# An AdaLN feed-forward kernel in split fp32r: the small transfers of pair 0 on GpSimd's queue, pair 0's blocks used in another order, and two reorderings on VectorE and ScalarE

## What is computed

```python
att = softmax(mlp(cond_128))                     # 64 x 8
agg_w = einsum('bk,koi->boi', att, weight)       # a 64 x 64 matrix per sample
y = einsum('boi,bih->boh', agg_w, x) + (att @ bias_k)[:, :, None]
scores = y @ gate_w.T + gate_b                   # 4 ranks
lora = y @ A[:r].T @ B[:, :r].T                  # r = the rank with the largest score
out = x + y @ W.T + b + lora
```

## Time and profile before

| | us |
|---|---|
| runs timed | 458.45, 458.93, 459.08 (median 458.93) |
| profiled execution, its time | 458.18 |
| its span on the core | 456.3 |
| PE busy | 450.4 (99%) |
| DVE busy | 343.8 (75%) |
| ACT busy | 181.4 (40%) |
| POOL busy | 19.4 (4%) |
| chain that ended last: PE, DVE, ACT | 96%, 3%, 1% |

### The profile page before, as it was taken

One profiled execution on the slowest core, in us unless ns is written; L12 is line 12 of the kernel. 1 busy time (PEld: TensorE's weight loads), 2 busy tenths in 40 slices (PEclk: granted clock), 3 DMA queues, 4 the chain that ended last, 5 costly groups with the idle time before them and its releaser, 6 DMA issues.

```text
span 456.3 us, 10477 instructions
## 1 busy us (share of the span) xinstructions
PE 450.4 (99%) x3510; PEld 445.8 (98%) x3510; DVE 343.8 (75%) x889; ACT 181.4 (40%) x415; POOL 19.4 (4%) x46
## 2 busy tenths in 40 slices
PE   9999999899999999999999999999999999999997
PEld 7999999899999999999999999999999999999997
DVE  4887988799586876958687695868769586876945
ACT  5654554455243343524334342433334243342511
POOL 1010000010000000000000000000000000100000
PEclk9999999999999999999999999999999999999999
DMA  7973560711608053250805235080523408052202
GB/s 273 344 277 54 145 227 1 239 46 52 232 1 278 6 188 97 88 195 0 281 1 194 88 90 192 0 278 4 201 81 108 174 5 277 0 190 95 92 2 93
DMA packets 23773, 59.18 MB, mean 130 GB/s; under 512 B 6862, under 2 KB 8834, under 8 KB 23684
## 3 DMA queue, kind: packets, MB, share of 16 engines
q1 hardware_dynamic: 23508, 58.78, 39.0%
q10 hardware_dynamic: 240, 0.07, 0.1%
HBM read 40.69 MB, written 18.15 MB: 129 GB/s over the span
## 4 chain that ended last, share of the span: by engine, by line
PE 96%; DVE 3%; ACT 1%; issue 0%; POOL 0%; ACTq 0%; POOLq 0%
PE p_p L1071 74%; PE p_o L1089 4%; PE p_o L1091 4%; PE p_o L1109 3%; PE p_o L1090 3%; PE p_o L1108 3%; PE p_p L1115 1%; PE p_p L1136 1%; PE p_p L1097 1%; PE p_o L1136 1%; DVE wl L716 1%; DVE w_raw L722 1%; DVE zl L792 0%; DVE aggw L776 0%; DVE prod L773 0%
## 5 line engine op out<-in xcount | busy, mean ns | idle before, releaser
L1071 PE MATMUL p_p<-wh,xh 128*128 128x274 f32 (+1 forms) x880 | 256.6, 292 | 0.0
L1071 PE MATMUL p_p<-wh,xl 128*128 128x274 f32 (+1 forms) x880 | 254.2, 289 | 0.0
L1071 PE MATMUL p_p<-wl,xh 128*128 128x272 f32 (+1 forms) x864 | 250.5, 290 | 0.0
L1071 PEld LDWEIGHTS p_p<-wh,xh 128*128 128x128 f32 x880 | 166.5, 189 | 0.4 <-issue 0.4
L1071 PEld LDWEIGHTS p_p<-wh,xl 128*128 128x128 f32 x880 | 166.7, 189 | 0.1
L1071 PEld LDWEIGHTS p_p<-wl,xh 128*128 128x128 f32 x864 | 163.0, 189 | 0.1
L579 ACT ACTIVATE zh<-sv 128x274 fp32r<-128x274 f32 (+1 forms) x56 | 24.3, 433 | 95.0 <-DVE sv L804 95.0
L811 DVE TENSOR_TENSOR xin<-p_o,xin 128x274 f32<-128x274 f32 (+2 forms) x128 | 52.0, 418 | 2.7 <-PE p_o L1109 1.9
L557 ACT ACTIVATE xh<-s_raw 128x512 fp32r<-128x512 f32 x60 | 36.3, 628 | 17.1 <-DVE s_raw L759 16.4
L579 ACT ACTIVATE zh<-p_p 128x272 fp32r<-128x272 f32 (+1 forms) x44 | 17.5, 398 | 60.7 <-PE p_p L1071 59.0
L766 DVE TENSOR_TENSOR xl<-s_raw,xh 128x512 fp32r<-128x512 f32 x60 | 40.9, 682 | 0.1
(11 more groups left out here) (140 smaller groups left out, 508.4 us busy)
## 6 DMA issues: line engine op xcount, KB each, us to landing
xin<-in_x SPq DMA_DIRECT2D x32, 512.0 KB, 4.0
raw<-in_xt SPq DMA_DIRECT2D x31, 512.0 KB, 5.2
out<-xin SPq DMA_DIRECT2D x30, 512.0 KB, 5.9
w_raw<-in_w SPq DMA_DIRECT2D x8, 274.0 KB, 7.0
w_raw<-in_w SPq DMA_DIRECT2D x8, 272.0 KB, 6.0
g_aggw<-aggw_all SPq DMA_DIRECT2D x8, 128.0 KB, 2.4
aggw<-g_aggw SPq DMA_DIRECT2D x15, 64.0 KB, 5.0
out<-xin SPq DMA_DIRECT2D x4, 137.0 KB, 2.1
```

Source lines behind the costliest of these rows:

```text
L1071: last = nc.tensor.matmul(o[:, 0:W[r]], a, m, start=start and p == 0, stop=stop and p == 2, skip_group_check=True)
```

## The change

**a. Pair 0 on PE and the weights' order.** The first round's blocks come as B12, B22, B11, B21. Its units stand so that each A block with the same weight block follows at once: `first_unit` B12, `other_unit`, `first_unit` B22, `attention_rows`, `other_unit`, `first_unit` B11 with `attention_products` in its middle, `other_unit`, `first_unit` B21; then the mixes of Z12 and Z22, the last unit, the mix of Z11, and round 1's first two units before the mix of Z21. The two `keep_busy(2)` inside the first `first_unit`s go. Column sums 0 and 1 swap.

**b. Transfers.** All 28 small ones are issued by POOL; SP's loads of `raw` are split in halves and `kern_s` comes before `kern`.

**c. ACT's and DVE's lists of pair 0** follow the new order; `kern_h` moves from DVE to ACT.

**d. Pair 2 on DVE.** `t_sum(0, R11)` comes before `bd_lo` of tile 1, and `z_lo` of Z11 right behind that, ahead of the residual and of the second `t_sum`.

**e. The end on PE.** The last mix and lora (Z21) are written out so that only the matmul with `zl` follows `z_lo`.

```diff
-        W_ORDER = [(r, n, h) for r in range(2) for n in (B11, B21, B12, B22) for h in range(2)]
+        W_ORDER = [(r, n, h) for r, blocks in enumerate(((B12, B22, B11, B21), (B11, B21, B12, B22)))
+                   for n in blocks for h in range(2)]
...
 # POOL
+            pool.wait_ge(s_kern_hl, 2)
+            for n, rows in enumerate((kern_h, kern_l)):
+                pool.dma_start(g_kern[n].rearrange("k (a n) -> (k a) n", n=KC), rows[:, :].bitcast(F32)).then_inc(s_k_stored, 16)
+            pool.wait_ge(s_aggbt, 1)
...
             u_bias(0, 0)
             u_bias(0, 1)
+            pool.wait_ge(s_k_stored, 16 * 2)
+            for h in range(HALVES):
+                for g, n in enumerate((0, 1, 0, 0)):
+                    row = (h * GROUPS + g) * K
+                    pool.dma_start(k_rows[row:row + K, :].bitcast(F32),
+                                 g_kern[n][:, h * KHALF:(h + 1) * KHALF]).then_inc(s_k_rows, 16)
+            pool.wait_ge(s_b_lo, 1)
+            for n, rows in enumerate((b_h, b_l)):
+                pool.dma_start(g_b[n].rearrange("(a o) -> a o", o=P), rows).then_inc(s_b_stored, 16)
+            sum_rows(0)
+            sum_rows(1)
+            pool.wait_ge(s_b_stored, 16 * 2)
+            pool.dma_start(bt_l[ROW_BH:ROW_BL + 1, :].bitcast(F32), g_b).then_inc(s_rows[0], 16)
+            sum_rows(2)
+            sum_rows(3)
...
 # DVE, pair 0
+            w_lo(6)
             mixing_weights(0)
+            w_lo(7)
+            z_lo(0, 0, 0, Z12)
             mixing_weights(1)
+            bd_lo(0, 0, 0)
+            z_lo(0, 0, 0, Z22)
+            bd_lo(0, 0, 1)
             cs_lo(0)
...
+            cs_lo(1)
+            z_lo(0, 0, 0, Z11)
...
 # PE, pair 0
                 if kk % 2 == 0:
-                        if at < 2:
-                            keep_busy(2)
                         pe.wait_ge(s_wl, at + 1)
...
-            first_unit(0, 0, 0)
+            first_unit(0, 2, 0, 0)
             pe.wait_ge(s_al, 2)
-            first_unit(0, 0, 1)
+            other_unit(0, 1, 0)
+            pe.wait_ge(s_al, 3)
+            first_unit(0, 2, 1, 1)
             attention_rows()
-            pe.wait_ge(s_al, 3)
-            first_unit(0, 1, 0, attention_products)
             pe.wait_ge(s_al, 4)
-            first_unit(0, 1, 1)
-            other_unit(0, 2, 0)
-            other_unit(0, 2, 1)
+            other_unit(0, 1, 1)
+            first_unit(0, 0, 0, 2, attention_products)
             other_unit(0, 3, 0)
-            mix(0, 0, 0, Z11)
-            other_unit(0, 3, 1)
-            pe.wait_ge(s_cs_lo, 2)
-            mix(0, 0, 0, Z22)
+            first_unit(0, 0, 1, 3)
             pe.wait_ge(s_aggbt, 2)
             pe.wait_ge(s_aggb, 1)
             mix(0, 0, 0, Z12)
-            first_unit(1, 0, 0)
-            first_unit(1, 0, 1)
+            pe.wait_ge(s_cs_lo, 1)
+            mix(0, 0, 0, Z22)
+            other_unit(0, 3, 1)
+            mix(0, 0, 0, Z11)
+            first_unit(1, 0, 0, 4)
+            first_unit(1, 0, 1, 5)
+            pe.wait_ge(s_cs_lo, 2)
             mix(0, 0, 0, Z21)
...
 # DVE, step
+                if two:
+                    t_sum(0, R11, R12, R11)
                 bd_lo(i, j, 1)
+                if two:
+                    z_lo(i, j, 0, Z11)
                 if not one:
                     residual(i, j - 1, 1, Z21)
                 if two:
-                    t_sum(0, R11, R12, R11)
                     t_sum(0, R12, R22, R12)
...
 # PE, the end
+            pe.wait_ge(s_zh, piece(*last, 1, Z21))
+            pe.wait_ge(s_y, piece(*last, 1, Z21 - 4))
+            nc.tensor.matmul(o, bd[:, 1, 0, :], zh[:, 1, zs], start=True, stop=False)
+            nc.tensor.matmul(o, bd[:, 1, 1, :], zh[:, 1, zs], start=False, stop=False)
+            nc.tensor.matmul(o, ut_hl[:, mine], bt_h[:, cols], start=False, stop=False)
+            nc.tensor.matmul(o, ut_h1[0:ROWS, mine], bt_l[0:ROWS, cols], start=False, stop=False)
+            pe.wait_ge(s_zl, piece(*last, 1, Z21))
+            nc.tensor.matmul(o, bd[:, 1, 0, :], zl[:, 1, zs], start=False, stop=True).then_inc(s_lora, 1)
```

More of the change, by code:

```diff
@@ L321, in piece, with made, z_place @@
             return count(i, j, PIECES, 4 * r + n)
+        def made(i, j, r, n):
+            return piece(i, j, r, MADE[n] if is_pair(i, j, 0) and r == 0 else n)
+        def z_place(i, j, r, n):
+            return (made(0, 0, 0, n) if is_pair(i, j, 0) and r == 0 else n) % 2 ^ 1
         def a_count(i, j, n):
@@ L401, in mixing_weights @@
                 sp.dma_start(aggw[:, :, :], g_aggw_pair[i * 2 + j]).then_inc(s_aggw_in, 16)
+            for t in range(4):
+                sp.dma_start(xin[:, t, :], x_t[t]).then_inc(s_x_in[t], 16)
             sp.wait_ge(s_g_stored, 16 * 3)
             gate_rows(0, 0)
[L405 to L422, removed]
             for n in range(KCH):
@@ L571, in z_hi @@
                 if early(i, j, r) or n == Z11:
-                    act.wait_ge(s_z, product(i, j, r, n if early(i, j, r) else P2))
+                    act.wait_ge(s_z, product(i, j, r, made(0, 0, 0, n) if is_pair(i, j, 0) and r == 0
+                                             else n if early(i, j, r) else P2))
                     src = {Z11: pa, Z22: pb, Z12: pc, Z21: pd}[n][:, 0:W[r]]
@@ L606, in _ @@
             w_hi(1)
+            act.wait_ge(s_raw_a21_in, 16)
+            nc.scalar.activation(a21h[:, :], raw[:, 1, 0:HB], ACT.Copy).then_inc(s_x1h, 1)
             act.wait_ge(s_sm, 4)
@@ L612, in _ @@
             act.wait_ge(s_raw_in[1], 16)
-            nc.scalar.activation(a21h[:, :], raw[:, 1, 0:HB], ACT.Copy).then_inc(s_x1h, 1)
             nc.scalar.activation(xh[:, A22, :], raw[:, 1, HB:H], ACT.Copy).then_inc(s_x1h, 1)
-            for m in range(4, 10):
-                w_hi(m)
+            w_hi(4)
+            w_hi(5)
+            act.wait_ge(s_kern_s_in, 16)
+            nc.scalar.activation(kern_h[:, :], kern_s[:, :], ACT.Copy).then_inc(s_kern_hl, 1)
+            z_hi(0, 0, 0, Z12)
+            w_hi(6)
+            w_hi(7)
+            z_hi(0, 0, 0, Z22)
             cs_hi(0)
-            z_hi(0, 0, 0, Z11)
+            w_hi(8)
+            w_hi(9)
             act.wait_ge(s_clear, 5)
@@ L988, in step @@
                     s_lo(i, j, S3)
-                z_lo(i, j, 0, Z11)
+                if not two:
+                    z_lo(i, j, 0, Z11)
                 if one:
@@ L1354, with blocks @@
     low = (half + 3) // 4 * 2
[L1356 to L1358 removed]
+    def blocks(cols, halves):
+        parts = [wag[k:k + kh, :, c + cols.start:c + cols.stop] for c in halves for k in (0, kh)]
         return np.stack([np.reshape(w, (2, kh // 2, P, -1)).transpose(0, 2, 1, 3) for w in parts])
@@ L1369 @@
         "bias_k": layer["bias_k"],
-        "w0": blocks(slice(low, half)),
-        "w1": blocks(slice(0, low)),
+        "w0": blocks(slice(low, half), (half, 0)),
+        "w1": blocks(slice(0, low), (0, half)),
         "b": ffn["b"],
```

153 lines of the change are left out of this document (73 added, 80 removed).

## The result

The changed kernel takes 462.63 us (median of 6 runs, 461.62 to 464.48) against 458.69 (6 runs, 458.40 to 459.20): a ratio of 1.0091, 95% interval 1.0066 to 1.0115. It is slower by 3.9 us, and PE waits where the prediction said; the sizes of the terms came out otherwise. Its profiled execution took 461.90 us with a span of 459.9, 3.6 us more than before. Single executions of one kernel differ by some us, and their granted clocks differ with them; that turns out to be part of the story.

The account below looks back on a forecast made before the run. PE, busy 99% of the span, was taken to bound the kernel. 458.18 + 0.2 (start) + 7.3 (transfers) + 1.0 (clock) - 1.4 (pair 2) - 0.5 (end) = 464.8; with 0.75 to the median, 465.5 us, range 457.0 to 471.0.

Parts of the forecast that it names:

- The place: POOL's queue held by `u_bias(0, 1)` to 34.53; PE waits about 7 us at the first `lora`, near 43.3.
- The direction: Whole kernel: slower with chance 0.62, faster 0.28, within 0.2% 0.10.
- c: Time for POOL to issue one small transfer, taken as 0.82 us.
- POOL as slow as SP's mean or a little more: Rival: c from 0.45 to 0.57, stall of 0.7 to 2.7 us, 457.9 to 459.9, no change; chance 0.13.
- The prediction's formula: PE's stall at the first `lora` is 17c - 7.0 us, for 17 transfers issued one after the other.
- a term of 7.3: Small transfers on POOL: 6.9 us stall at the first `lora` plus 0.4 for the last `sum_rows` transfers.
- one rival only: POOL issues as fast as SP's quick rows: no `lora` stall, `k_rows` up to 0.9 us late, 457.2 to 458.1; chance 0.27.
- The further rows: Last 6 `sum_rows` transfers come 4.9 us later, PE needs them 4.5 us behind the first `lora`: 0.4 more.
- The clock: PE may run slower behind the stall: +1.0 us, between 0 and 4.6, with half pace for 7.5 to 9.3 us at most.
- The start: Pair 0: fillers' removal gains 0.9, three short waits cost 1.75 in place of 0.8: +0.2 us, from -0.9 to +1.5.
- Pair 2: `zl` ends before PE asks, so the stall before the mix goes whole: -1.4 us.
- The end: Four matmuls move ahead of PE's wait for the last `zl`: -0.5 us.

Follow-up runs that it names:

- The experiment with one moved line: Changed kernel with `u_bias(0, 1)` moved behind the small transfers on POOL instead of ahead of them: 456.10 us, ratio 0.9942 to the kernel before.
- the profiles with the fillers: Changed kernel with 6 unread matmuls on PE ahead of its `k_rows` wait and 7 ahead of the first `lora`'s rows: 459.99 us.
- with `g_b` first: Changed kernel with the two `g_b` transfers issued ahead of the eight `k_rows` on POOL instead of behind them: 462.60 us.
- the first experiment: Changed kernel with all 28 small transfers back on SP, in the order of the kernel before: 461.39 us, ratio 1.006 to the kernel before.
- both kernels with part b alone: Kernel before with its 28 small transfers on POOL: 464.37 us in the changed kernel's order, 460.69 us with `u_bias(0, 1)` behind them.
- the pair of SP orders: Changed kernel with its 28 transfers on SP: 461.39 us in the order of the kernel before, 456.21 us with `g_kern` first and `k_rows` early.

## Why the prediction was right, and where its terms were off

**The place** was right. The queue is held by `u_bias(0, 1)` until `route` has ended (34.70 + 0.48, forecast 34.53), PE waits at the rows for the first `lora`, the clock falls behind it. Not all of the wait is there: 1.5 of the 3.3 us fall on `k_rows`. The experiment with one moved line shows the cause. The time, 462.6, lies under the 465.5 forecast.

**The direction** was right in part by luck. The forecast of a slower kernel had the condition that c lies above 0.57, and c is 0.505. That is inside the rival *POOL as slow as SP's mean or a little more* (0.45 to 0.57, chance 0.13, 457.9 to 459.9, no change). With the measured c the prediction's own terms give 458.93 + 0.2 + 1.6 - 1.9 = 458.8, and with its 1.0 for the clock 459.8. What made the kernel slower all the same is what the sum didn't have: the round trip, 1.8, the later start of the queue, 0.6, and a clock that cost more.

**Issue time c** was mis-sized: 0.50 us for each transfer where 0.82 was taken, 4.08/8 for `k_rows`, 0.50 for a csx row. POOL's pace at arithmetic said nothing about its pace at issuing, and SP's mean of 0.44 was the nearest row by far. The prediction's formula gives 17 × 0.505 - 7.0 = 1.6 us of stall with it. By the estimate from the Trainium skill's page DMA: Bandwidth & Descriptors, c = 0.84, the stall would have been 7.3; the trace doesn't bear out that the later first byte is paid once for each transfer on the engine.

**A round trip was missing** from the same sum. It let 17 transfers go out back to back; the last but for `sum_rows(2)` and `(3)` reads `g_b` back from DRAM, and POOL waits 1.78 us for the write. The rest is small: the first `k_rows` goes out 0.6 later than forecast (in this execution; in the profiles with the fillers and with `g_b` first the first transfer goes out at 34.4), the last transfer lands 1.4 after its issue instead of 1.8, and PE itself comes 0.2 later. 1.6 + 1.8 + 0.6 - 0.4 - 0.2 = 3.4, as measured. Two errors of opposite sign, -5.4 for c and +1.8 for the round trip, met in a term of 7.3.

**`k_rows` lands 5 us after its last issue** (39.24 to 44.39), and this made the first of the two waits. The prediction had it as a matter of up to 0.9 us in one rival only, and that figure was too small: its rows give 34.53 + 2.82 = 37.35 for the end of the issuing at SP's pace, not 36.9, and so up to 1.5. It moved nothing in the sum, since the `lora`'s rows came later still, but where `g_b` went first it became the bound.

**The further rows** of `sum_rows(2)` and `(3)` cost nothing (0.4 forecast): issued by 48.5, needed near 53.4. From the first `lora` to that mix are 5.0 us in the kernel before (43.13 to 48.11), not 4.5.

**The clock** cost 1.5 us in the profiled execution, 1.0 forecast. The half pace lasted 3.5 us, not the 7.5 to 9.3 of the upper bound. It needed no 7 us of idle: waits of 1.5 and 1.8 us with 0.7 of work between were enough, and in the kernel with d and e one of 1.17. But waits of 1.20 (the first experiment), 1.25 (and as much in both kernels with part b alone) and 1.68 us (the kernel with d and e, up to 28.16, for DVE) left it at 1.00. What decides between these isn't settled here.

**The start** gave +0.4 for a forecast of +0.2, with three delays near 24 to 28.5 as described (0.5 and 0.5 in the waits, a smaller one at 24.70), and about 0.25 in place of the 0.9 for the fillers: PE is ready for the first mix at 24.45, not 23.8. One pair of executions can't carry a number this small. PE comes to full pace early in one execution and late in another, here in the changed kernel and in the one with the moved line:

```profile
9.48 0.43 PE L1100 MATMUL p_p<-wh,xh 128*128 128x272 f32 x1
```

```profile
6.17 0.28 PE L1100 MATMUL p_p<-wh,xh 128*128 128x272 f32 x1
```

The clock column says 1.00 in both; the pace shows it, one matmul every 0.23 us against 0.125. Round 1 of pair 0 begins between 28.26 and 28.99 in the seven profiles with the changed order on PE and DVE, and between 27.30 and 28.61 in the four with the order of the kernel before. So whether the new start gains or loses isn't shown.

**Pair 2** gave -1.5 for -1.4. **The end** gave -0.5 at PE's last matmul for -0.5, and 0.1 in the span.

**The baseline** was the hidden error. The prediction took the wait of zero at `k_rows` in the profiled execution before as the state of the kernel. It seems to be one of two, with SP's rows arriving at the edge. That the 460s of the kernel before are late rows is argued, from the profile of the kernel with d and e, the pair of SP orders and the granted clocks; no such execution of the kernel before itself was profiled.

The Trainium skill's rule (Trainium Kernel Development and Optimization, Key Constraints) that queues of several engines share the 16 DMA engines and save only issuing time agrees with 456.2 on SP and 456.1 and 456.3 on POOL in the same kind of order.

## What to carry to other kernels

When short transfers move to another engine's queue, look first at what that engine waits for ahead of them: here one operation, needed only a pair later, held 17 transfers for some 7 us. Price a chain of transfers by its round trips through DRAM and its landings as well as by issue times, and put the transfer that another one reads back first. A wait of PE costs more than its length where the clock falls behind it, so where single runs of a kernel spread and their granted clocks with them, look for a wait that only some executions meet; the one that was profiled may not have it. Compare two profiles by distances from a common landmark, since their starts can differ by 0.7 us and more.

## What the hardware showed unexpectedly

- POOL issues a `k_rows`, `g_b` or csx transfer in 0.48 to 0.55 us, whether it has 8 rows of 8 KB or one short row (the two `g_kern` ones took 0.76 and 0.56), and SP the same ones mostly in 0.23 to 0.82.
- The same 4 KB to `g_b` took 7.3 us from issue to landing behind the `k_rows` while the DMA engines were full, 3.5 behind them later, and 1.6 ahead of them.
- PE waits of 1.17 to 2.8 us were followed by some 3.5 us at 1.2 GHz in four profiled executions and by 7 in a fifth, while single waits of 1.20 to 1.25 us in four places and of 1.68 us in one were not. Matmuls whose result nobody reads, put into the wait, kept the clock at 2.4 GHz and gave back 1.5 us in the profile and 2.6 by the median.
- At the start of the kernel PE came to full pace at about 5 us in one execution and at 9.9 in another.
